# Attention probabilities transposed by DMA instead of on TensorE

## The chip, the cores and the metric

The kernel runs on all 8 cores of one Trainium2 chip. Each core computes a quarter of the sequence (1024 tokens, with 64 tokens of its neighbours on each side) of one of two batch items; the cores exchange nothing. The time is that of the slowest core on the device, in microseconds (us). The engines of a core are named as the profile names them: PE (TensorE), DVE (VectorE), ACT (ScalarE), POOL (GpSimd) and SP (SyncE, which here only issues DMAs).

## The reference

Layer normalisation, banded attention with learned sinks, and a gated feed-forward block that reads the same normalised input; the result is x + s * silu(ffn). What matters here is the attention (32 heads of 64, windows of 64, 16 sinks a head):

```python
s_band = jnp.einsum('bhnqd,bhnkd->bhnqk', Qb, Kband) * scale
s_band = jnp.where(mask, s_band, -jnp.inf)
s_sink = jnp.einsum('bhnqd,hsd->bhnqs', Qb, sinks) * scale
p = jax.nn.softmax(jnp.concatenate([s_sink, s_band], axis=-1), axis=-1)
O = jnp.einsum('bhnqs,hsd->bhnqd', p[..., :S], sinks) \
  + jnp.einsum('bhnqk,bhnkd->bhnqd', p[..., S:], Vband)
```

## The kernel before

It runs in stages, with a barrier between them: normalisation and transposing of the input, projection of q, k and v, attention, feed-forward (gate, up and down products over weights streamed from HBM), output projection and final addition.

The attention stage is a loop over 128 pairs (c, qt): c names two heads, A and B, that lie in the two halves of the partitions, and qt a tile of 128 queries. For each pair the scores of 128 queries against 16 sinks and 256 keys go to psA and psB (p3_emit_scores, three matmuls a head, L542 to L547). VectorE takes their maxima (L597, L598). ScalarE forms the exponentials into pA_bf and pB_bf (bf16, 128 queries on the partitions by 272 columns) and their sums (L620, L623). VectorE inverts the sums and scales the probabilities (L601 to L605). For the product with v the probabilities must have the keys on the partitions, so TensorE transposes them in six pieces into ps_tp: two of 128 x 128 and one of 128 x 16 (sinks) a head (p3_emit_tp, L556 to L561). VectorE copies them to SBUF, the wide pieces to pt_sb (L608, L609) and the sinks' to pts_sb (L610, L611). Six matmuls give the output (p3_emit_av, L573 to L577), and ScalarE evicts it to o_buf (L629, L631). After every eighth pair SP stores o_buf to DRAM (p3_sync). Buffers are double.

The order is written out by hand. TensorE has: scores of pairs 0 and 1, then for each i the transposes of i, the output of i, the scores of i + 2. ScalarE has for each i the exponentials of i and then the evictions of i; VectorE has the maxima, the scalings and the copies of i. The engines meet through three counting semaphores: TS is raised by TensorE, VS by VectorE, SS by ScalarE. `ts_tp[i]`, `vs_nm[i]` (scaled), `vs_pt[i]` (copied), `ts_av[i]` and `ss_oe[i]` (evicted) are their values for pair i. DMAs have semaphores of their own, wrapped by the class Slots, whose `dma` (L37) issues every DMA. The feed-forward stage's weights are loaded by POOL, which waits for the last store of the attention stage.

Of the kernel before, what the change touches and what calls it, by code (L numbers as in the profile page):

```python
# [8 lines left out]
BF16 = mybir.dt.bfloat16  # L9
# [10 lines left out]
NT_OWN = TOK // 128  # L20
DH = 64
NH = 32
NS = 16
# [64 lines left out]
def build_program2():  # L88
    nc = bass.Bass("TRN2", target_bir_lowering=False)
# [20 lines left out]
    d_oscr = nc.dram_tensor("o_scr", [16, 128, 1024], BF16, kind="Internal").ap()  # L110
# [10 lines left out]
    with ExitStack() as glob:  # L121
        eg = glob.enter_context
        ctx = Ctx(nc, glob)
# [6 lines left out]
        id_bf = eg(nc.sbuf_tensor("id_bf", [128, 128], BF16))  # L130
# [140 lines left out]
        with ExitStack() as sA:  # L271
# [209 lines left out]
            o_buf = [ea(nc.sbuf_tensor(f"o_buf{i}", [128, 1024], BF16)) for i in range(2)]  # L481
            pA_bf = [ea(nc.sbuf_tensor(f"pA_bf{i}", [128, 272], BF16)) for i in range(2)]
            pB_bf = [ea(nc.sbuf_tensor(f"pB_bf{i}", [128, 272], BF16)) for i in range(2)]
            pt_sb = [ea(nc.sbuf_tensor(f"pt_sb{i}", [128, 512], BF16)) for i in range(2)]
            pts_sb = [ea(nc.sbuf_tensor(f"pts_sb{i}", [NS, 256], BF16)) for i in range(2)]
# [6 lines left out]
            OS = Slots(nc, glob, "os", 2)  # L492
            OS_outer[0] = OS

            pairs = [(c, qt) for c in range(16) for qt in range(NT_OWN)]
            NP3 = len(pairs)
# [4 lines left out]
            vs_nm = [0] * NP3  # L501
            ts_tp = [0] * NP3
            vs_pt = [0] * NP3
            ts_av = [0] * NP3
            ss_oe = [0] * NP3
            ostok = [None] * 16
# [17 lines left out]
            for i in range(NP3):  # L524
# [5 lines left out]
                c, qt = pairs[i]  # L530
# [19 lines left out]
            def p3_emit_tp(t, i):  # L550
                ctx.wait(t, "VS", vs_nm[i])
                if i >= 2:
                    ctx.wait(t, "VS", vs_pt[i - 2])
                pt = ps_tp[i % 2]
                pa, pb = pA_bf[i % 2], pB_bf[i % 2]
                t.transpose(pt[:, 0:128], pa[:, NS:NS + 128], id_bf[:])  # L556
                t.transpose(pt[:, 128:256], pa[:, NS + 128:NS + 256], id_bf[:])
                t.transpose(pt[0:NS, 256:384], pa[:, 0:NS], id_bf[:])
                t.transpose(pt[:, 384:512], pb[:, NS:NS + 128], id_bf[:])
                t.transpose(pt[:, 512:640], pb[:, NS + 128:NS + 256], id_bf[:])  # L560
                ins = t.transpose(pt[0:NS, 640:768], pb[:, 0:NS], id_bf[:])  # L561
                ctx.inc(ins, "TS")

            def p3_emit_av(t, i):
                c, qt = pairs[i]
                ctx.wait(t, "VS", vs_pt[i])
                if i >= 1:
                    ctx.wait(t, "SS", ss_oe[i - 1])
                for hh in range(2):
                    h = 2 * c + hh  # L570
                    pav = ps_oA if hh == 0 else ps_oB
                    co = hh * 256
                    t.matmul(pav[:], v_t[:, qt, h * 64:(h + 1) * 64],  # L573
                             pt_sb[i % 2][:, co:co + 128], start=True, stop=False)
                    t.matmul(pav[:], v_t[:, qt + 1, h * 64:(h + 1) * 64],
                             pt_sb[i % 2][:, co + 128:co + 256], start=False, stop=False)
                    ins = t.matmul(pav[:], sinkn_bf[:, h * 64:(h + 1) * 64],  # L577
                                   pts_sb[i % 2][:, hh * 128:hh * 128 + 128],
                                   start=False, stop=True)
                ctx.inc(ins, "TS")  # L580

            def p3_tensor(t):
                MS.wait_all(t)
                for kind, i in tseq:
                    if kind == "sc":
                        if i >= 2:
                            ctx.wait(t, "SS", ss_ex[i - 2])
                        p3_emit_scores(t, i)
                    elif kind == "tp":
                        p3_emit_tp(t, i)  # L590
                    else:
                        p3_emit_av(t, i)

            def p3_vector(v):
                for i in range(NP3):
                    ctx.wait(v, "TS", ts_sc[i])
                    v.reduce_max(nmA[i % 2][:], psA[i % 2][:], axis=AX, negate=True)  # L597
                    ctx.inc(v.reduce_max(nmB[i % 2][:], psB[i % 2][:], axis=AX,  # L598
                                         negate=True), "VS")
                    ctx.wait(v, "SS", ss_ex[i])  # L600
                    v.reciprocal(rcA[i % 2][:], rsA[i % 2][:])  # L601
                    v.reciprocal(rcB[i % 2][:], rsB[i % 2][:])
                    v.drain()
                    v.tensor_scalar_mul(pA_bf[i % 2][:], pA_bf[i % 2][:], rcA[i % 2][:])  # L604
                    ctx.inc(v.tensor_scalar_mul(pB_bf[i % 2][:], pB_bf[i % 2][:],  # L605
                                                rcB[i % 2][:]), "VS")
                    ctx.wait(v, "TS", ts_tp[i])
                    v.tensor_copy(pt_sb[i % 2][:, 0:256], ps_tp[i % 2][:, 0:256])  # L608
                    v.tensor_copy(pt_sb[i % 2][:, 256:512], ps_tp[i % 2][:, 384:640])  # L609
                    v.tensor_copy(pts_sb[i % 2][:, 0:128], ps_tp[i % 2][0:NS, 256:384])  # L610
                    ctx.inc(v.tensor_copy(pts_sb[i % 2][:, 128:256],  # L611
                                          ps_tp[i % 2][0:NS, 640:768]), "VS")

            def p3_scalar(sc):
                for i in range(NP3):
                    c, qt = pairs[i]
                    ctx.wait(sc, "VS", vs_mx[i])
                    if i >= 2:
                        ctx.wait(sc, "TS", ts_tp[i - 2])
                    sc.activation(pA_bf[i % 2][:], psA[i % 2][:], AF.Exp,  # L620
                                  bias=nmA[i % 2][:], scale=1.0,
                                  accum_out=rsA[i % 2][:])
                    ctx.inc(sc.activation(pB_bf[i % 2][:], psB[i % 2][:], AF.Exp,  # L623
                                          bias=nmB[i % 2][:], scale=1.0,
                                          accum_out=rsB[i % 2][:]), "SS")
                    ctx.wait(sc, "TS", ts_av[i])
                    if qt == 0 and c >= 2:
                        OS.wait(sc, ostok[c - 2])
                    sc.activation(o_buf[c % 2][0:64, qt * 128:(qt + 1) * 128],  # L629
                                  ps_oA[:], AF.Copy)  # L630
                    ctx.inc(sc.activation(o_buf[c % 2][64:128, qt * 128:(qt + 1) * 128],  # L631
                                          ps_oB[:], AF.Copy), "SS")

            def p3_sync(s):
                for c in range(16):
                    last_i = c * NT_OWN + (NT_OWN - 1)
                    ctx.wait(s, "SS", ss_oe[last_i])
                    tok = OS.dma(s, d_oscr[c], o_buf[c % 2][:], c % 2)
                    assert tok == ostok[c]

            with ExitStack() as sP3:
                psA = [sP3.enter_context(nc.psum_tensor(f"psA{i}", [128, 272], F32))
                       for i in range(2)]
                psB = [sP3.enter_context(nc.psum_tensor(f"psB{i}", [128, 272], F32))
                       for i in range(2)]
                ps_tp = [sP3.enter_context(nc.psum_tensor(f"ps_tp{i}", [128, 768], BF16))
                         for i in range(2)]
                ps_oA = sP3.enter_context(nc.psum_tensor("ps_oA", [64, 128], F32))
                ps_oB = sP3.enter_context(nc.psum_tensor("ps_oB", [64, 128], F32))
                block.tensor(p3_tensor)  # L650
                block.vector(p3_vector)
                block.scalar(p3_scalar)
                block.sync(p3_sync)
                assert ctx.cnt["TS"] == cTS and ctx.cnt["VS"] == cVS
                assert ctx.cnt["SS"] == cSS
# [425 lines left out]
```

## Time and profile before

| | us |
|---|---|
| median of 3 runs | 3245.32 |
| lowest and highest | 3132.2, 3301.79 |
| the profiled execution | 3131.45 |
| its span, slowest core (core 1) | 3129.9 |
| spans of the 8 cores | 3076.9 to 3129.9 |
| PE busy | 2464.7 (79%) |
| DVE busy | 801.7 (26%) |
| ACT busy | 536.9 (17%) |
| POOL busy | 136.8 (4%) |

The profile is one execution. A line such as "1260.04 0.28 PE ps_oA L573" in the chain of work that ended last says that from 1260.04 us on, for 0.28 us, the chain ran through the matmul of line 573 that writes ps_oA; "issue" in it is time in which an engine waited for nothing that the profile shows. An instruction that overlaps the one before it is counted in the chain only from where the former ends, so its figure there can be smaller than its duration.

### The profile page before, as it was taken

To read this page: it belongs to the slowest core of one execution; us is meant where nothing else is said; L and a number is where in the kernel's file an instruction comes from. 1 tells how busy PE (TensorE), PEld (TensorE's weight loads), DVE (VectorE), ACT (ScalarE), POOL (GpSimd) and SP (SyncE) were. 2 spreads that over 40 slices of the span, in tenths; PEclk is the share of its full clock that TensorE was granted. 3 is DMA by queue.
4 is the path that set the end of the run, shared out by engine and by line. 5 is a ranking of instruction groups with operands and counts; after the bars stand their busy time and mean duration, and the time that the engine had idled before them with its cause. 6 is when DMAs were issued, how large, how long until landed. Compare 5 with 4: busy or idle time off the path is not lost.

```text
span 3129.9 us, 32762 instructions; the slowest of 8 cores (3076.9 to 3129.9 us)
## 1 busy us (share of the span) xinstructions
PE 2464.7 (79%) x11816; PEld 1126.9 (36%) x11816; DVE 801.7 (26%) x2289; ACT 536.9 (17%) x1362; POOL 136.8 (4%) x259
## 2 busy tenths in 40 slices
PE   2387776995555555555599999999999999999796
PEld 1133222772222222222244444444444444444343
DVE  4344333002333333333203121120303121211224
ACT  3244333212222222222100000000000000000010
POOL 0000000000000000000010000101010100000000
PEclk9999888995555555555599999999999999999895
DMA  2233113221000000000254353617152443524445
GB/s 96 76 54 51 30 34 54 41 41 13 4 7 4 7 4 7 4 7 7 39 86 68 68 94 54 108 33 117 26 96 52 75 87 60 102 48 88 115 75 188
DMA packets 50747, 174.03 MB, mean 56 GB/s; under 512 B 9872, under 2 KB 11040, under 8 KB 46368
## 3 DMA queue, kind: packets, MB, share of 16 engines
q0 software_dynamic: 41616, 135.04, 25.4%
q1 hardware_dynamic: 8976, 36.91, 3.4%
q8 instruction: 100, 1.64, 0.2%
q14 instruction: 55, 0.45, 0.1%
HBM read 294.36 MB, written 12.58 MB: 98 GB/s over the span
## 4 chain that ended last, share of the span: by engine, by line
PE 59%; ACT 11%; DVE 11%; DMA 9%; issue 7%; DVEq 1%; POOL 1%; ACTq 0%; SPq 0%; POOLq 0%
PE ps_d L773 15%; PE ps_g L747 11%; PE ps_u L759 11%; DMA wd_ib<-wd_pack 6%; PE ps_v L424 4%; PE ps_s L911 3%; PE ps_qk L355 3%; ACT pA_bf L620 2%; ACT pB_bf L623 2%; DVE t L388 1%; DVE m L391 1%; ACT t2sw L372 1%; DVE pA_bf L604 1%; ACT t2sw L371 1%; ACT t2sw L369 1%
## 5 line engine op out<-in xcount | busy, mean ns | idle before, releaser
L773 PE MATMUL ps_d<-h_ib,wd_ib 128*128 128x512 bf16 x2048 | 458.3, 388 | 35.5 <-DMA wd_ib<-wd_pack 35.5
L747 PE MATMUL ps_g<-xn_f,gbuf 128*128 128x512 bf16 x2048 | 465.1, 380 | 10.3 <-DMA gbuf<-wgu_pack 10.3
L759 PE MATMUL ps_u<-xn_f,ubuf 128*128 128x512 bf16 x2048 | 462.9, 379 | 0.0
L355 PE MATMUL ps_qk<-xn_f,wbuf 128*128 128x512 bf16 (+1 forms) x1280 | 285.4, 381 | 121.2 <-DVE k_f L393 74.9
L773 PEld LDWEIGHTS ps_d<-h_ib,wd_ib 128*128 128x128 bf16 x2048 | 203.6, 100 | 290.0 <-issue 58.8
L798 DVE TENSOR_TENSOR h_ib<-tg,ps_u 128x512 bf16<-128x512 f32 x128 | 88.0, 688 | 811.5 <-PE ps_u L759 811.5
L747 PEld LDWEIGHTS ps_g<-xn_f,gbuf 128*128 128x128 bf16 x2048 | 200.8, 98 | 253.5 <-issue 13.3
L788 ACT ACTIVATE tg<-ps_g 128x512 f32<-128x512 f32 x128 | 76.4, 597 | 1238.4 <-PE ps_g L747 1238.4
L759 PEld LDWEIGHTS ps_u<-xn_f,ubuf 128*128 128x128 bf16 x2048 | 200.4, 98 | 241.6
L808 DVE TENSOR_TENSOR g_sb<-g_sb,ps_d 128x512 f32<-128x512 f32 x224 | 154.0, 687 | 275.6 <-PE ps_d L773 275.6
L355 PEld LDWEIGHTS ps_qk<-xn_f,wbuf 128*128 128x128 bf16 x1280 | 118.6, 104 | 273.8 <-issue 189.4
L556 PE MATMUL ps_tp<-id_bf,pA_bf 128*128 128x128 bf16 x128 | 34.0, 266 | 194.9 <-DVE pB_bf L605 194.9
L573 PE MATMUL ps_oA<-pt_sb,v_t 128*64 128x128 bf16 x128 | 36.4, 284 | 146.3 <-DVE pts_sb L611 146.3
L424 PE MATMUL ps_v<-vbuf,xn_f 128*128 128x256 bf16 x1152 | 139.6, 275 | 2.8 <-ACT v_t L436 2.8
L629 ACT ACTIVATE o_buf<-ps_oA 64x128 bf16<-64x128 f32 x128 | 34.7, 271 | 606.2 <-PE ps_oB L577 606.2
L911 PE MATMUL ps_s<-o_sb,wobuf 128*128 128x512 bf16 x512 | 112.3, 382 | 21.4 <-DMA o_sb<-o_scr 20.8
L424 PEld LDWEIGHTS ps_v<-vbuf,xn_f 128*128 128x128 bf16 x1152 | 107.5, 98 | 23.6 <-issue 3.0
L37 POOL DMA_DIRECT2D gbuf<-wgu_pack x64 | 33.9, 530 | 1852.3 <-PE ps_g L747 1014.5
L601 DVE RECIPROCAL rcA<-rsA 128x1 f32<-128x1 f32 x128 | 20.9, 163 | 339.5 <-ACT pB_bf L623 339.5
L223 PE MATMUL ps_tr<-id_bf,xn_bf 128*128 128x128 bf16 x144 | 29.1, 264 | 95.9 <-ACT xn_bf L212 74.4
L556 PEld LDWEIGHTS ps_tp<-id_bf,pA_bf 128*128 128x128 bf16 x128 | 13.3, 104 | 228.7 <-issue 228.7
L597 DVE TENSOR_REDUCE nmA<-psA 128x1 f32<-128x272 f32 x128 | 53.7, 419 | 160.1 <-PE psB L547 160.1
(104 smaller groups left out, 2206.4 us busy)
## 6 DMA issues: line engine op xcount, KB each, us to landing
gbuf<-wgu_pack POOLq DMA_DIRECT2D x64, 512.0 KB, 6.1
ubuf<-wgu_pack POOLq DMA_DIRECT2D x64, 512.0 KB, 5.9
wd_ib<-wd_pack POOLq DMA_DIRECT2D x64, 512.0 KB, 18.1
u_buf<-u_ext SPq DMA_DIRECT2D x17, 1024.0 KB, 6.8
wbuf<-wqkv_pack POOLq DMA_DIRECT2D x32, 512.0 KB, 5.1
vbuf<-v_pack POOLq DMA_DIRECT2D x8, 1024.0 KB, 8.4
wobuf<-wo_pack POOLq DMA_DIRECT2D x16, 512.0 KB, 5.1
out<-out_buf SPq DMA_DIRECT2D x8, 1024.0 KB, 4.7
```

The costliest lines, as they stand in the source:

```text
L355: t.matmul(p[:, 0:ln], wbuf[oc % 2][:, kc * 128:(kc + 1) * 128], src[:, kc, :], start=(kc == 0), stop=False)
L424: t.matmul(p[:], xn_f[:, kc, tt * 128:(tt + 1) * 128], vbuf[gp % 2][:, kc * 256:(kc + 1) * 256], start=(kc == 0), stop=False)
L597: v.reduce_max(nmA[i % 2][:], psA[i % 2][:], axis=AX, negate=True)
L620: sc.activation(pA_bf[i % 2][:], psA[i % 2][:], AF.Exp, bias=nmA[i % 2][:], scale=1.0, accum_out=rsA[i % 2][:])
L623: ctx.inc(sc.activation(pB_bf[i % 2][:], psB[i % 2][:], AF.Exp, bias=nmB[i % 2][:], scale=1.0, accum_out=rsB[i % 2][:]), "SS")
L747: ins = t.matmul(pg[:], gbuf[ic % 2][:, kc * 128:(kc + 1) * 128], xn_f[:, kc, HALO + tsx * 512:HALO + (tsx + 1) * 512], start=(kc == 0), s ...
L759: ins = t.matmul(pu[:], ubuf[ic % 2][:, kc * 128:(kc + 1) * 128], xn_f[:, kc, HALO + tsx * 512:HALO + (tsx + 1) * 512], start=(kc == 0), s ...
L773: ins = t.matmul(pd[:], wd_ib[:, ic, oc * 128:(oc + 1) * 128], h_ib[:, ic, tsx * 512:(tsx + 1) * 512], start=(ic == 0), stop=(ic == 7))
L788: ctx.inc(sc.activation(tg[gi % 2][:], ps_g[gi % 2][:], AF.Silu), "SS")
L798: ctx.inc(v.tensor_mul(h_ib[:, ic, tsx * 512:(tsx + 1) * 512], tg[gi % 2][:], ps_u[gi % 2][:]), "VS")
L808: ins = v.tensor_add(dst, dst, ps_d[j % 2][:])
L911: ins = t.matmul(p[:], wobuf[oc % 2][:, kc * 128:(kc + 1) * 128], o_sb[:, kc, tsx * 512:(tsx + 1) * 512], start=(kc == 0), stop=(kc == 15))
```

## The change

The wide transposes leave TensorE and become DMAs. In p3_emit_tp only the two sink pieces are left, and ps_tp shrinks to 16 x 256. VectorE copies only those two. SP's p3_sync, which had only the stores, now waits in every pair for the scaled probabilities and for the output matmuls of two pairs back, and issues four `dma_start_transpose` of 128 x 128 bf16 each, from pA_bf and pB_bf straight to pt_sb, both in SBUF. Each raises the semaphore of its buffer (PT, one for each of the two buffers) by 16. TensorE waits for 64 more on it before the output matmuls, and ScalarE before it overwrites pA_bf and pB_bf two pairs later. The store of every eighth pair stands behind that pair's transposes in SP's order.

```diff
--- before.py
+++ after.py
@@ -553,17 +553,14 @@
                     ctx.wait(t, "VS", vs_pt[i - 2])
                 pt = ps_tp[i % 2]
                 pa, pb = pA_bf[i % 2], pB_bf[i % 2]
-                t.transpose(pt[:, 0:128], pa[:, NS:NS + 128], id_bf[:])
-                t.transpose(pt[:, 128:256], pa[:, NS + 128:NS + 256], id_bf[:])
-                t.transpose(pt[0:NS, 256:384], pa[:, 0:NS], id_bf[:])
-                t.transpose(pt[:, 384:512], pb[:, NS:NS + 128], id_bf[:])
-                t.transpose(pt[:, 512:640], pb[:, NS + 128:NS + 256], id_bf[:])
-                ins = t.transpose(pt[0:NS, 640:768], pb[:, 0:NS], id_bf[:])
+                t.transpose(pt[:, 0:128], pa[:, 0:NS], id_bf[:])
+                ins = t.transpose(pt[:, 128:256], pb[:, 0:NS], id_bf[:])
                 ctx.inc(ins, "TS")
 
             def p3_emit_av(t, i):
                 c, qt = pairs[i]
                 ctx.wait(t, "VS", vs_pt[i])
+                PT.wait(t, pttok[i])
                 if i >= 1:
                     ctx.wait(t, "SS", ss_oe[i - 1])
                 for hh in range(2):
@@ -605,11 +602,9 @@
                     ctx.inc(v.tensor_scalar_mul(pB_bf[i % 2][:], pB_bf[i % 2][:],
                                                 rcB[i % 2][:]), "VS")
                     ctx.wait(v, "TS", ts_tp[i])
-                    v.tensor_copy(pt_sb[i % 2][:, 0:256], ps_tp[i % 2][:, 0:256])
-                    v.tensor_copy(pt_sb[i % 2][:, 256:512], ps_tp[i % 2][:, 384:640])
-                    v.tensor_copy(pts_sb[i % 2][:, 0:128], ps_tp[i % 2][0:NS, 256:384])
+                    v.tensor_copy(pts_sb[i % 2][:, 0:128], ps_tp[i % 2][:, 0:128])
                     ctx.inc(v.tensor_copy(pts_sb[i % 2][:, 128:256],
-                                          ps_tp[i % 2][0:NS, 640:768]), "VS")
+                                          ps_tp[i % 2][:, 128:256]), "VS")
 
             def p3_scalar(sc):
                 for i in range(NP3):
@@ -617,6 +612,7 @@
                     ctx.wait(sc, "VS", vs_mx[i])
                     if i >= 2:
                         ctx.wait(sc, "TS", ts_tp[i - 2])
+                        PT.wait(sc, pttok[i - 2])
                     sc.activation(pA_bf[i % 2][:], psA[i % 2][:], AF.Exp,
                                   bias=nmA[i % 2][:], scale=1.0,
                                   accum_out=rsA[i % 2][:])
@@ -631,19 +627,43 @@
                     ctx.inc(sc.activation(o_buf[c % 2][64:128, qt * 128:(qt + 1) * 128],
                                           ps_oB[:], AF.Copy), "SS")
 
+            PT = Slots(nc, glob, "pt", 2)
+            pttok = [None] * NP3
+            ptc = [0, 0]
+            for i in range(NP3):
+                for _ in range(4):
+                    ptc[i % 2] += 16
+                pttok[i] = (i % 2, ptc[i % 2])
+
             def p3_sync(s):
-                for c in range(16):
-                    last_i = c * NT_OWN + (NT_OWN - 1)
-                    ctx.wait(s, "SS", ss_oe[last_i])
-                    tok = OS.dma(s, d_oscr[c], o_buf[c % 2][:], c % 2)
-                    assert tok == ostok[c]
+                next_store = 0
+                for i in range(NP3):
+                    c, qt = pairs[i]
+                    ctx.wait(s, "VS", vs_nm[i])
+                    if i >= 2:
+                        ctx.wait(s, "TS", ts_av[i - 2])
+                    pa, pb = pA_bf[i % 2], pB_bf[i % 2]
+                    dst = pt_sb[i % 2]
+                    s.dma_start_transpose(dst[:, 0:128], pa[:, NS:NS + 128]).then_inc(
+                        PT.sems[i % 2], 16)
+                    s.dma_start_transpose(dst[:, 128:256], pa[:, NS + 128:NS + 256]).then_inc(
+                        PT.sems[i % 2], 16)
+                    s.dma_start_transpose(dst[:, 256:384], pb[:, NS:NS + 128]).then_inc(
+                        PT.sems[i % 2], 16)
+                    s.dma_start_transpose(dst[:, 384:512], pb[:, NS + 128:NS + 256]).then_inc(
+                        PT.sems[i % 2], 16)
+                    PT.cnt[i % 2] += 64
+                    if qt == NT_OWN - 1:
+                        ctx.wait(s, "SS", ss_oe[i])
+                        tok = OS.dma(s, d_oscr[c], o_buf[c % 2][:], c % 2)
+                        assert tok == ostok[c]
 
             with ExitStack() as sP3:
                 psA = [sP3.enter_context(nc.psum_tensor(f"psA{i}", [128, 272], F32))
                        for i in range(2)]
                 psB = [sP3.enter_context(nc.psum_tensor(f"psB{i}", [128, 272], F32))
                        for i in range(2)]
-                ps_tp = [sP3.enter_context(nc.psum_tensor(f"ps_tp{i}", [128, 768], BF16))
+                ps_tp = [sP3.enter_context(nc.psum_tensor(f"ps_tp{i}", [NS, 256], BF16))
                          for i in range(2)]
                 ps_oA = sP3.enter_context(nc.psum_tensor("ps_oA", [64, 128], F32))
                 ps_oB = sP3.enter_context(nc.psum_tensor("ps_oB", [64, 128], F32))
```

## Rows read from the trace of the kernel before

**Rows 1.** Stretches: PE, PEld, DVE, ACT, POOL busy us (instructions); granted clock; DMA share, GB/s.

```profile
723.45:1535.60 812.15, 473.20 (x2292) 192.87 (x2292) 274.13 (x1274) 202.24 (x764) 0.00 (x0) 0.50 0.01 5
...
1545.20:2926.60 1381.40, 1344.46 (x6144) 604.84 (x6144) 264.11 (x384) 78.25 (x130) 99.43 (x189) 0.98 0.42 73
```

**Rows 2.** Line 556: count, duration ns min/median/max, first and last start in us.

```profile
L556 PE MATMUL ps_tp<-id_bf,pA_bf x128: 262/266/266, 723.5 to 1531.5; 128*128 128x128 bf16 x128
```

**Rows 3.** Chain that ended last, one pair: start us, us on it, what.

```profile
1253.74 0.29 PE ps_oA L573
...
1255.06 0.07 ACT o_buf L629
...
1255.64 0.58 ACT pA_bf L620 x2
...
1257.38 0.21 DVE pB_bf L605
1257.59 0.24 issue
1257.83 0.27 PE ps_tp L556
...
1259.05 0.15 DVE pt_sb L608
...
1259.66 0.14 DVE pts_sb L611
1259.80 0.24 issue
1260.04 0.28 PE ps_oA L573
```

**Rows 4.** The same chain at the attention stage's end.

```profile
1535.27 0.28 ACT o_buf L631
...
1535.61 2.03 DMA o_scr<-o_buf
...
1545.10 0.14 issue
1545.23 1.01 PE ps_g L747 x2
```

**Rows 5.** Order of time on SP's queue: start us, duration us, what is issued.

```profile
125.43 0.33 SPq L37 DMA_DIRECT2D cq_t<-cq  x1
125.81 0.42 SPq L37 DMA_DIRECT2D sq_t<-sq  x1
126.28 0.42 SPq L37 DMA_DIRECT2D ck_t<-ck  x1
126.74 0.43 SPq L37 DMA_DIRECT2D sk_t<-sk  x1
```

**Rows 6.** Order of time on POOL: issue of a load in small pieces.

```profile
709.36 0.63 POOL L37 DMA_DIRECT2D sinkn_bf<-sinks_n  x1
```

**Rows 7.** DMA issues: count, KB each, median us from issue to landing.

```profile
o_scr<-o_buf SPq DMA_DIRECT2D x16, 256.0 KB, 2.0
...
sinkt_bf<-sinks_t POOLq DMA_DIRECT2D x2, 64.0 KB, 4.0
id_f<-ident SPq DMA_DIRECT2D x1, 64.0 KB, 1.8
...
consts_sb<-consts SPq DMA_DIRECT2D x1, 2.0 KB, 1.8
```

**Rows 8.** SP's issues in the attention stage (first start us, time to the last's end).

```profile
771.92 764.01 SPq L37 DMA_DIRECT2D o_scr<-o_buf  x16
```

**Rows 9.** DMA busy tenths in 40 slices of 771.90 to 773.00 us.

```profile
DMA  0000000000000000000000000000013795597995
```

**Rows 10.** DMA busy tenths in 40 slices of 773.00 to 775.00 us.

```profile
DMA  9799997942200000000000000000000000000000
```

**Rows 11.** DMA queue 0 from 706 to 710.5 us: packets, MB, share of 16 engines.

```profile
q0 software_dynamic: 2389, 0.08, 82.7%
```

## The prediction

> **What bounds the kernel now.** I looked first at the spans of all cores. They lie between 3076.9 and 3129.9 us, and both dies have a clock of 0.833, so the slowest core speaks for all. Then I looked at the page's slices, which show a stretch of about ten slices, from about 720 to 1540 us, in which TensorE is half busy and its clock is down. Busy times by stretch give it exactly [rows 1]: from 723.45 to 1535.60 us TensorE is busy 473.20 of 812.15 us, VectorE 274.13, ScalarE 202.24, and the 16 DMA engines 1% of the time. The granted clock is 0.50, the lower of the two levels (1.2 GHz). In the feed-forward stretch behind it, it is 0.98, near the upper one. That first stretch is the attention loop that the diff edits. No engine is full in it and no transfer is, so it is bound by a chain of waits.
>
> The first transposes (L556) of the 128 pairs start from 723.5 to 1531.5 us [rows 2]; 808.0 / 127 is 6.36 us a pair. The chain that ended last shows what a pair consists of [rows 3]: the output matmuls start at 1253.74 and those of the next pair at 1260.04, 6.30 us later. In between come, one behind the other: six output matmuls, two evictions on ScalarE, two exponentials (from 1255.64), two reciprocals and two scalings on VectorE (to 1257.59), six transposes on TensorE (from 1257.83), four copies on VectorE (1259.05 to 1259.80), and the next output matmuls at 1260.04. The exponentials of a pair stand behind the evictions of the pair before in ScalarE's order, so nothing of the next pair's softmax runs ahead: each microsecond added between scaling and output matmul is added 128 times.
>
> **The change, part by part.** The piece that is replaced runs from the end of the scaling, 1257.38 + 0.21 = 1257.59, to the output matmul at 1260.04: 2.45 us [rows 3]. The other 3.85 us of the pair stay. I call the new length of this piece D.
>
> *Removed:* four of six transposes on TensorE and the two wide copies (L608, L609). *Kept:* the two transposes of the sink columns and two small copies. They start 0.24 us behind the scaling as now and are through in well under 2.45 us, since they are a subset of what takes 2.45 us today. They run beside the DMAs, so I cost them at nothing; if the DMAs were through at once, they would be the chain. VectorE's maxima of the next pair move ahead of the output matmul; they aren't on the chain today, so that gives nothing. TensorE's clock is at its lower level already and TensorE only gets less to do, so I let every matmul time stand and the feed-forward stage start as before.
>
> *Added:* SP waits for the scaling, issues four transposing DMAs of 32 KB (128 x 128 bf16) from SBUF to SBUF, and TensorE waits for all four before the output matmuls. Its terms:
>
> - SP's start behind the engine that it waits for: the eviction L631 ends at 1535.27 + 0.28 = 1535.55, SP's store starts at 1535.61: 0.06 us [rows 4].
> - Three issue spacings ahead of the fourth. Four plain loads stand back to back on SP at 125.43, 125.81, 126.28 and 126.74 us: 1.31 us for three, 0.44 each [rows 5]. The trace has no transposing DMA. The dearest issue near it is POOL's of a load in small pieces, 0.63 us [rows 6]. That is another queue's way of making descriptors, but a transpose is also cut into small pieces, so I take 0.63, which makes 1.89; the low end is 1.31.
> - The landing of the fourth, from its issue. The store of 256 KB takes 2.03 us [rows 4] and 16 of them have a median of 2.0. Loads of 64 KB and of only 2 KB take 1.8, so size is hardly in it; a 64 KB load in small pieces takes 4.0 [rows 7]. A transpose has smaller pieces than the store (rows of 256 bytes) and larger ones than that load (64 bytes), and a reordering on top. I take 2.7, nearer to the store; the ends are 2.03 and 4.0.
> - TensorE's start behind a DMA: 0.14 us, rounded to 0.13 where the chain counts to the matmul [rows 4].
>
> D is then 0.06 + 1.89 + 2.7 + 0.13 = 4.78 us. That is 2.33 us more than 2.45, and times 128 it is 298 us. At the low end, D is 0.06 + 1.31 + 2.03 + 0.13 = 3.53, +1.08 a pair, +138 us. At the high end, with 0.63 and 4.0, D is 6.08, +3.63, +465 us.
>
> *Stores.* SP's 16 stores of o_buf now stand in the order between the transposes. The first store issues at 771.92 [rows 8], just as ScalarE begins the next pair's exponentials; from there to the end of the next scaling it is 1257.59 - 1255.64 = 1.95 us [rows 3]. The next issue could follow after 0.44 us [rows 5], so the store is out of the way; without that cover it would cost 16 x 0.44 = 7 us. SP's wait for the output matmuls two pairs back is always met by then. ScalarE's new wait, for the transposes two pairs back, is met too, since those output matmuls have run. What stands behind TensorE's new wait are the output matmuls and the scores two pairs on, whose buffers are a pair ahead. POOL's feed-forward loads wait for the last store and so start later by just what the loop grows.
>
> The profiled execution is 3131.45 us (its span 3129.9), and I sum against it: 3131 + 298 = 3429 us. The median of the runs shown is 3245.32 and the lowest 3132.2, so the profiled one is among the fastest; I forecast for executions like it, and the range has room for a median that is some tens of us above.
>
> The Trainium skill, Advanced Engine Details and Errata, section X-Bar Transpose (TRN2), says that a transposing DMA on this chip is as fast as a plain one. By it D would be the low end above; no row here shows one.
>
> **Rivals.**
>
> *1. The four transposes run one behind the other.* In the sum they overlap and only their issues are apart. If the path that reorders takes one at a time and holds it for t, D is 0.06 + 4t + 0.13 at least. For t there is only a bound: a whole landing each, 2.03 us [rows 4], which gives D = 8.31, +5.86 a pair, +750 us: 3881 us. The middle between 0.44 (the spacing of plain issues, below which it has no effect) and 2.03 is 1.24; it gives D = 5.15, +346 us, 3477 us. It overtakes my forecast's D of 4.78 from t = 1.15 us on. For it: all four use the same engines and one queue. Against it: pieces pass quickly. 2389 small packets took 82.7% of 16 engines over 4.5 us [rows 11], that is 59.5 us of engine time or 25 ns each, and a transpose has 128 rows, 8 for an engine, 0.2 us.
> The Trainium skill, VectorE: DVE Perf Modes, section The three transpose paths, gives 1309 ns for a 128 x 128 bf16 transpose by DMA and 390 ns on TensorE. If that is what each holds the path for, D would be an estimated 5.4 us and the time about 3510 us, between forecast and rival. TensorE's own figure isn't met here: one such transpose (L556) has a median of 266 ns [rows 2].
>
> *2. It isn't slower.* What is transposed is 32 KB and never leaves SBUF, and four transposes on TensorE and two copies are gone from the chain. The first store's packets begin at about 772.70 and end at about 773.55 [rows 9, 10], so of the 2.03 us that follow its issue at 771.92 [rows 8] some 0.85 are data; 1.2 us are left for a transfer without any. With spacings of 0.44, D is 0.06 + 1.31 + 1.2 + 0.13 = 2.70, +0.25 a pair, +32 us: 3163 us, which can't be told from no change. It decides at D = 2.94, where 0.49 x 128 is 2%; for a gain of 2%, D would have to be 1.96, which four issues of 0.44 leave only 0.46 for. Against it: a load of 2 KB, almost no data, still took 1.8 us [rows 7].
>
> *3. The transposes move single elements.* 16384 elements at 25 ns over 16 engines [rows 11] are 25.6 us for one, 102 us a pair, and the kernel would take over 16000 us. A milder form, a piece of 32 bytes at a time (1024 pieces, 1.6 us each, in series), gives D = 0.06 + 6.4 + 1.2 + 0.13 = 7.8 us and falls together with rival 1. For the single elements only the layout speaks: source neighbours land on different partitions.
>
> **How the numbers follow.** The forecast's mechanism (issues apart, landings overlapping, D from 3.53 to 6.08): 3269 to 3596 us, chance 0.60. Rival 1, t from 1.15 to 2.03, 3430 to 3881 us: 0.25, of which two fifths for t below 1.4. Rival 3 or anything beyond: 0.07. Rival 2: 0.08, of which 0.02 for faster. The range of 3265 to 3890 us takes in the first two, 0.85. A change of under about 2% can't be told from none, so: faster 0.02, within 2% 0.06, slower 0.92. The likeliest case gives 3429 us.
>
> **What the profile after would show.** The period of L573 or of the first transpose: 8.6 us a pair instead of 6.3, with the stretch at 1110 us instead of 812. The output matmul's idle time should be ended by a DMA, about 3.5 us or more of it a pair. In SP's order, four issues a pair 0.44 to 0.63 us apart. If they are 1.2 us or more apart, or the landing grows from the first transpose to the fourth, it is rival 1 (or the issue itself is the bound, which my 0.63 would have missed). Evictions, exponentials and scalings should have their old durations and the feed-forward stretch its 1381 us. If the output matmul's wait is still ended by the small copies (now L607), rival 2 holds. The forecast is wrong above all if the issue or the landing of a transposing DMA is unlike a plain one's: each 0.1 us in a spacing is worth 3 x 0.1 x 128 = 38 us, each 0.1 us in the landing 13 us.

## The result, and the profile after

The changed kernel is slower. Its median is 3628.17 us over 9 runs (lowest 3610.22); the ratio to the kernel before is 1.159, with a 95% interval of 1.155 to 1.163. The profiled execution took 3610.22 us, 479 us more than the profiled one of before (3131.45). The forecast was 3429 us: the right direction and the right place, but 298 us of growth instead of 479. In some executions of both kernels, and in all three of the one with eight DMAs below, the cores of one die were slowed, which lifts the plain medians (before: 3242.11 over 10 runs); the ratios, and the times quoted below for every kernel but that one, leave those executions out.

The waits of the changed kernel on its slowest core (who waited for whom: us in total, times, longest) have one new row at TensorE. It answers to the 146.3 us that the output matmul waited for VectorE's copies before:

```profile
PE ps_oA L570 <- DMA pt_sb<-pB_bf: 747.2, 128, 6.9
```

The lines that answer to [rows 1] are busy times by stretch of the changed kernel, the attention loop and the feed-forward stage (PE, PEld, DVE, ACT, POOL, granted clock, DMA share and GB/s):

```profile
729.00:2049.60 1320.60, 378.75 (x1780) 151.95 (x1780) 224.09 (x1022) 201.49 (x764) 0.00 (x0) 0.50 0.07 16
2058.00:3405.00 1347.00, 1332.81 (x6144) 601.59 (x6144) 263.49 (x384) 77.70 (x129) 99.44 (x188) 1.00 0.42 75
```

The loop grew from 812 to 1321 us with less work in it, at the same granted clock of 0.50. The 16 DMA engines are busy 7% of it, so it isn't the data.

The chain that ended last, through one pair of the changed kernel, answers to [rows 3] (start us, us on the chain, what):

```profile
1257.14 1.10 SPq L647
1258.23 0.04 issue
1258.28 1.23 SPq L649
1259.51 0.04 issue
1259.55 1.23 SPq L651
1260.78 0.04 issue
1260.83 2.33 DMA pt_sb<-pB_bf
1263.16 0.40 issue
1263.55 0.28 PE ps_oA L570
```

The scaling of this pair ends at 1257.03. SP starts 0.11 us later, holds its queue for 1.10 us with the first transposing DMA and for 1.23 us with each further one, and can start the fourth only at 1260.83. That one lands 2.33 us later. From scaling to output matmul it is 1263.55 - 1257.03 = 6.52 us, against 2.45 us before. The first of the four already holds the queue for 1.10 us, when those of the pair before have long landed (the output matmul of that pair started at 1253.18): so the hold belongs to the issue itself, and waiting for an earlier transpose can be at most the 0.13 us by which the others are dearer.

Over the whole loop: the tile pt_sb of the changed kernel lists, for each instruction that writes or reads it, the duration (min/median/max ns) and the first and last start:

```profile
L647 SPq DMA_TRANSPOSE pt_sb<-pA_bf x128: 1093/1095/1174, 730.3 to 2041.0; - x128
L649 SPq DMA_TRANSPOSE pt_sb<-pA_bf x128: 1214/1232/2350, 731.6 to 2042.1; - x128
L651 SPq DMA_TRANSPOSE pt_sb<-pB_bf x128: 1095/1232/2301, 732.8 to 2043.4; - x128
L653 SPq DMA_TRANSPOSE pt_sb<-pB_bf x128: 1226/1232/1236, 734.1 to 2045.7; - x128
...
L570 PE MATMUL ps_oA<-pt_sb,v_t x128: 283/286/288, 736.6 to 2048.3; 128*64 128x128 bf16 x128
...
DMA to landing us min/median/max: 2.2/2.3/4.9
```

The output matmul's first and last starts give (2048.3 - 736.6) / 127 = 10.33 us a pair, 3.97 more than the 6.36 of [rows 2], so 508 us in 128 pairs. Most pairs take 10.2 to 10.3 us; single ones take up to 11.3, some of them where an issue is held for about 2 us (the largest values of L649 and L651). The rest of the difference lies outside the loop: the first scaling ends at 730.24 instead of 723.35 us (the masks' load took 12.6 instead of 7.6 us), +7, and the feed-forward stretch took 1347 instead of 1381 us, -34. These are two different cores: the slowest of before (core 1) lost 35.5 us to late wd_ib loads, the slowest of after (core 6) 11.8 us; and TensorE was busy 11.7 us less in the stretch, at a granted clock of 1.00 instead of 0.98. 508 + 7 - 34 = 481, measured 479.

### The profile page after: what moved, and what is told of

The parts are those of the page before. It is cut to its first block, busy times and chain, and to the rows that moved or that the text cites. A ratio compares the mean times of both kernels' runs of the same rounds, so it can differ in the third digit from the quotient of the medians.

```text
span 3608.7 us, 32502 instructions; the slowest of 8 cores (3575.1 to 3608.7 us)
## 1 busy us (share of the span) xinstructions
PE 2360.8 (65%) x11304; PEld 1082.4 (30%) x11304; DVE 752.3 (21%) x2033; ACT 536.0 (15%) x1362; POOL 136.8 (4%) x259
## 3 DMA queue, kind: packets, MB, share of 16 engines
q1 hardware_dynamic: 90896, 53.75, 5.2%
## 4 chain that ended last, share of the span: by engine, by line
PE 49%; DMA 14%; SPq 13%; ACT 10%; DVE 8%; issue 5%; DVEq 1%; POOL 1%; ACTq 0%; POOLq 0%
PE ps_d L793 12%; PE ps_g L767 10%; PE ps_u L779 10%; DMA pt_sb<-pB_bf 8%; SPq L649 5%; SPq L651 4%; SPq L647 4%; PE ps_v L424 4%; DMA wd_ib<-wd_pack 3%; PE ps_s L931 3%; PE ps_qk L355 3%; ACT pA_bf L616 2%; ACT pB_bf L619 2%; DVE t L388 1%; DVE m L391 1%
## 5 line engine op out<-in xcount | busy, mean ns | idle before, releaser
L793 PE MATMUL ps_d<-h_ib,wd_ib 128*128 128x512 bf16 x2048 | 446.0, 381 | 13.9 <-DMA wd_ib<-wd_pack 11.8
L570 PEld LDWEIGHTS ps_oA<-pt_sb,v_t 128*64 128x64 bf16 x128 | 16.3, 127 | 779.2 <-issue 779.2
L556 PE MATMUL ps_tp<-id_bf,pA_bf 128*16 128x128 bf16 x128 | 33.9, 265 | 196.2 <-DVE pB_bf L602 196.2
L424 PEld LDWEIGHTS ps_v<-vbuf,xn_f 128*128 128x128 bf16 x1152 | 107.4, 98 | 23.7 <-issue 3.0
```

The lines of the kernel that those rows point to most:

```text
L424: t.matmul(p[:], xn_f[:, kc, tt * 128:(tt + 1) * 128], vbuf[gp % 2][:, kc * 256:(kc + 1) * 256], start=(kc == 0), stop=False)
L793: ins = t.matmul(pd[:], wd_ib[:, ic, oc * 128:(oc + 1) * 128], h_ib[:, ic, tsx * 512:(tsx + 1) * 512], start=(ic == 0), stop=(ic == 7))
```

## The experiments

The first question was what makes SP's issue three times as dear as a plain DMA's 0.44 us. Theory F says that the time is fixed for each transposing DMA, whatever its size. Theory T says that it grows with the number of 16 x 128 tiles in it. The second question was whether the chain of waits, and not an engine or a queue, makes the loop what it is in both kernels.

### Two wide DMAs for four

```diff
-  four s.dma_start_transpose of 128 x 128
+  s.dma_start_transpose(dst[:, 0:256].rearrange("p (a b) -> p a b", a=2), pa[:, NS:NS + 256])
+  s.dma_start_transpose(dst[:, 256:512].rearrange("p (a b) -> p a b", a=2), pb[:, NS:NS + 256])
```

> The changed kernel with the same data in two transposing DMAs of 128 x 256 for a pair instead of four of 128 x 128. Theory F, the time that a transposing DMA holds SP's queue (1.23 us) is fixed for each DMA: both still take about 1.2 us, one spacing of 1.27 us ahead of the last instead of three, the pair falls from 10.33 to about 7.8 us, the kernel to about 3290 us. Theory T, it grows with the tiles of 16 x 128 that a DMA holds (8 in the changed kernel, 16 here): each takes 2 to 2.5 us, the pair stays between 9.8 and 10.4 us, the kernel at about 3600 us.

Measured: 3322.62 us; a pair is (1726.6 - 730.4) / 127 = 7.84 us. The tile pt_sb in this kernel:

```profile
L647 SPq DMA_TRANSPOSE pt_sb<-pA_bf x128: 1152/1154/1401, 726.6 to 1722.7; - x128
L650 SPq DMA_TRANSPOSE pt_sb<-pB_bf x128: 1188/1216/2584, 727.9 to 1723.8; - x128
L570 PE MATMUL ps_oA<-pt_sb,v_t x128: 283/284/287, 730.4 to 1726.6; 128*64 128x128 bf16 x128
```

A DMA with twice the data holds SP's queue for about as long as before, 1.15 to 1.22 us on this core (core 1) and 1.17 to 1.25 us on the even ones; T wanted 2 us or more. Issues are a little dearer on even cores (see the last section), so the price of a spacing is taken between even ones: on core 6 a pair of this kernel is (1732.1 - 732.4) / 127 = 7.87 us, and (10.33 - 7.87) / 2 is 1.23 us for each spacing that is gone. F holds, T falls.

### One tile instead of eight

```diff
-  s.dma_start_transpose(dst[:, 0:128], pa[:, NS:NS + 128])            (and three more)
+  s.dma_start_transpose(dst[:, 0:16], pa[0:16, NS:NS + 128])          (and three more)
```

> The changed kernel with four transposing DMAs of one tile (16 x 128) each for a pair instead of eight tiles each; the other seven eighths of the probabilities are left out (zeros stand there), so its output is not the reference's. Theory F: each still holds SP's queue for 1.1 to 1.2 us, the pair stays at 10.3 us and the kernel at 3610 us. Theory T: the issue falls towards the 0.44 us spacing of a plain DMA, the pair to about 7.5 us, the kernel to about 3250 us.

Measured: 3620.47 us in the profiled execution and (2046.4 - 738.3) / 127 = 10.30 us a pair, with an eighth of the data:

```profile
L650 SPq DMA_TRANSPOSE pt_sb<-pA_bf x128: 1085/1087/1178, 732.1 to 2040.0; - x128
L652 SPq DMA_TRANSPOSE pt_sb<-pA_bf x128: 1197/1224/2356, 733.3 to 2041.1; - x128
...
DMA to landing us min/median/max: 2.2/2.3/3.5
```

With an eighth of the data the issue falls by only 0.01 us (1.09 and 1.22 against 1.10 and 1.23), and the landing doesn't. This is F from the other side.

### Plain copies in the same place

```diff
-  s.dma_start_transpose(dst[:, 0:128], pa[:, NS:NS + 128])            (and three more)
+  s.dma_start(dst[:, 0:128], pa[:, NS:NS + 128])                      (and three more)
```

> The changed kernel with each transposing DMA replaced by a plain copy of the same 128 x 128 block, SBUF to SBUF; the transposition of the wide blocks is left out, so its output is not the reference's. This prices the low end of the prediction. If only the transposing makes SP's issue dear: spacings of 0.44 us, landing of 1.6 to 2.0 us, D of about 3.5 us (from scaling to output matmul), the pair 7.3 us, the kernel 3260 us. If any short DMA in this place costs that much (its wait, or the SBUF source): spacing 1.2 us and 3550 us or more.

Measured: 3350.05 us, (1739.9 - 734.0) / 127 = 7.92 us a pair. The first lines are the tile pt_sb, the others one pair in order of time (start us, duration us):

```profile
L647 SPq DMA_DIRECT2D pt_sb<-pA_bf x128: 464/465/521, 730.2 to 1735.9; - x128
L649 SPq DMA_DIRECT2D pt_sb<-pA_bf x128: 574/587/873, 730.7 to 1736.4; - x128
...
DMA to landing us min/median/max: 1.7/1.8/3.0
```

```profile
1259.32 0.28 DVE L602 TENSOR_SCALAR pB_bf<-pB_bf,rcB 128x272 bf16<-128x272 bf16 x1
1259.73 0.46 SPq L647 DMA_DIRECT2D pt_sb<-pA_bf  x1
1260.24 0.58 SPq L649 DMA_DIRECT2D pt_sb<-pA_bf  x1
1260.87 0.58 SPq L651 DMA_DIRECT2D pt_sb<-pB_bf  x1
1261.49 0.59 SPq L653 DMA_DIRECT2D pt_sb<-pB_bf  x1
...
1263.58 0.28 PE L570 MATMUL ps_oA<-pt_sb,v_t 128*64 128x128 bf16 x1 [3.36 <-DMA pt_sb<-pB_bf]
```

Between the two cases of the expectation: spacings of 0.51, 0.63 and 0.62 us, 1.76 us for three, dearer than the 1.31 of the loads in [rows 5], and a landing of 1.8 us. From scaling to output matmul it is 3.98 us. So my middle value of 0.63 us for a spacing is what a plain SBUF to SBUF copy costs in this place; transposing adds 0.64 us to each spacing and 0.5 us to the landing. A landing is counted from the start of the issue. From the issue's end on it is 2.3 - 1.23 = 1.1 us for a transposing DMA and 1.8 - 0.59 = 1.2 us for a plain one: so what the transposing adds lies in the issue alone, and the landing is later because the issue is longer. Of the loop's +508 us, about (7.92 - 6.36) x 128 = 200 us would be there with plain copies, and about 308 us are the transposing.

### Half of the transposes back on TensorE

```diff
-  s.dma_start_transpose(dst[:, 256:384], pb[:, NS:NS + 128])  and its neighbour
+  t.transpose(pt[:, 256:384], pb[:, NS:NS + 128], id_bf[:])   and its neighbour
+  v.tensor_copy(pt_sb[i % 2][:, 256:512], ps_tp[i % 2][:, 256:512])
```

> The changed kernel with head B's two wide blocks transposed on TensorE and copied by VectorE as before, head A's two by DMA. If each issue costs 1.27 us on the chain: D falls by two spacings, 2.54 us, from 6.5 to 4.0 us, the pair to 7.8 us, the kernel to about 3285 us, and the output matmul still waits for a DMA. If the landing, not the issues, were what counts, the pair would stay above 9 us and the kernel above 3450 us.

Measured: 3319.14 us, (1723.4 - 730.8) / 127 = 7.82 us a pair; the output matmul still waits for a DMA:

```profile
PE ps_oA L572 <- DMA pt_sb<-pA_bf: 370.2, 128, 4.0
```

Two issues less are 10.33 - 7.82 = 2.51 us less, as two wide DMAs for four were 2.46 us less (core 6). Half of the data or all of it in two DMAs comes to the same.

### Eight DMAs for four

```diff
-  s.dma_start_transpose(dst[:, 0:128], pa[:, NS:NS + 128])            (and three more)
+  s.dma_start_transpose(dst[:, 0:64], pa[0:64, NS:NS + 128])
+  s.dma_start_transpose(dst[:, 64:128], pa[64:128, NS:NS + 128])      (and six more)
```

> The changed kernel with each transposing DMA cut into two of 64 rows by 128 columns, eight for a pair with the same data. Theory F (issue time fixed for each DMA): four more spacings of 1.27 us, the pair from 10.33 to about 15.4 us, the kernel to about 4260 us. Theory T (by the tile): the pair stays near 10.4 us.

Measured: 4341.56 us in the profiled execution; the rows are of core 5 (span 4217.4 us). The last of its eight issues and the output matmul:

```profile
L661 SPq DMA_TRANSPOSE pt_sb<-pB_bf x128: 1197/1198/1204, 736.3 to 2665.9; - x128
L570 PE MATMUL ps_oA<-pt_sb,v_t x128: 283/286/287, 738.8 to 2668.6; 128*64 128x128 bf16 x128
```

A pair is (2668.6 - 738.8) / 127 = 15.20 us; in the changed kernel an odd core needs 10.24 us (core 7: 733.1 to 2033.9). Four more issues are 4.96 us, 1.24 us each. From one tile to sixteen in a DMA, and from two to eight DMAs a pair, the time follows the number of DMAs, and their size hardly matters.

### One DMA a pair

Head B's sink columns go behind its keys, so that the 512 wide columns of both heads are one run in memory:

```diff
-  pA_bf, pB_bf: two tensors [128, 272], each sinks then keys
+  pAB_bf: one tensor [128, 544]: sinks A, keys A, keys B, sinks B
+  s.dma_start_transpose(dst[:].rearrange("p (a b) -> p a b", a=4), pAB_bf[i % 2][:, NS:NS + 512])
```

> The changed kernel with one transposing DMA of 128 x 512 for a pair (head B's sink columns moved behind its keys so that the source is one run; the computation is the same). Theory F (issue time fixed for each DMA): D is one landing and two wake-ups, about 2.8 us, the pair 6.7 us, the kernel about 3180 us. Theory T (issue time by the tile, 0.15 us each, 32 tiles here): the issue takes about 4.9 us, D stays at 6.3 us or more, the kernel at 3590 us.

> The changed kernel with one transposing DMA of 128 x 512 a pair, timed again in rounds against the kernel before. In the one profiled execution a pair took 6.77 us against 6.36 of before, +0.41 x 128 = 52 us, so a ratio of 1.015 to 1.025 is expected: the change's loss almost gone, but no gain.

Measured: 3198.81 us in one execution, (1590.4 - 730.0) / 127 = 6.77 us a pair. The chain of this kernel, one pair (start us, us on it, what):

```profile
1105.08 0.21 DVE pAB_bf L607
...
1105.41 2.42 DMA pt_sb<-pAB_bf
1107.84 0.24 issue
1108.08 0.29 PE ps_oA L575
```

No issue spacing is left. From scaling (1105.29) to output matmul it is 2.79 us, 0.34 more than the 2.45 us of TensorE and VectorE. The issue of 1.19 us is within the 2.42 us of landing; T wanted 4.9 us for it. The size isn't quite without effect: the first issue of a pair takes 1.087, 1.095, 1.169 and 1.190 us for DMAs of 1, 8, 16 and 32 tiles (medians on even cores), 0.10 us more for 32 times the data. In further runs the kernel took 3175.25 to 3198.22 us against 3128.95 and 3134.63 of before: a ratio of about 1.016. The loss is nearly gone and there is no gain. It also shows the limit of the theory that only SP's issues matter: with one DMA the path is still one landing long.

### The order changed alone

Theory: the loop is bound by its chain. Then the transposes' path is expensive only because nothing else is done meanwhile. I moved the work of neighbouring pairs into each other, first with all transposes on TensorE as before:

```diff
 for i in range(NP3):
     tseq.append(("tp", i))
-    tseq.append(("av", i))
+    if i >= 1: tseq.append(("av", i - 1))
     if i + 2 < NP3: tseq.append(("sc", i + 2))
+ VectorE: scale(i), maxima(i + 1), copies(i)
+ ScalarE: exponentials(i), evictions(i - 2)
```

> The kernel before with its order changed alone: TensorE runs the output matmuls of a pair behind the transposes of the next one, ScalarE the exponentials of a pair ahead of the evictions of two pairs back, VectorE the maxima of the next pair ahead of the copies. If the attention loop is bound by the chain of waits and not by an engine, the pair falls from 6.36 us to what TensorE is busy at the lower clock, 473 / 128 = 3.7 us, the stretch from 812 to about 480 us, the kernel to about 2800 us, lower if the clock rises. If an engine or the waits between engines bind it, it stays above 3000 us.

Measured: ratio 0.891 (0.887 to 0.895); runs of 2783.15 to 2796.45 us; (1191.5 - 731.9) / 127 = 3.62 us a pair. From 800 to 1100 us its chain is TensorE alone. The first lines are a part of that chain, from the scores of one pair over the transposes to the output of another; the second are the busy times of a stretch of the loop:

```profile
1003.23 0.23 PE psB L562
1003.45 0.22 PE ps_tp L571
...
1004.31 0.21 PE ps_tp L576
1004.52 0.24 PE ps_oA L588
```

```profile
800.00:1100.00 300.00, 300.00 (x1488) 125.18 (x1488) 185.43 (x826) 130.85 (x496) 0.00 (x0) 0.50 0.03 10
```

TensorE is busy 300.00 of 300 us. The old order was bound by its chain: same instructions, another order, 335 to 350 us less.

### The new order with the DMAs

> The changed kernel with the same new order, so that a pair's transposing DMAs fly while the next pair's softmax runs. If the loss of the change is the length of the DMA path on the chain and SP's queue is the next bound: the pair takes four spacings, about 5.15 us, less than the 6.36 of before; the kernel about 2990 us, faster than before by 4 to 5% but slower than the same order with transposes on TensorE. If the DMAs' latency can't be covered (buffers of the probabilities are given back only when they land), the pair is 8 us or more and the kernel above 3300 us.

The edit is that of the section above, made to the changed kernel; SP's stores also move back by two pairs. Measured: ratio 0.951 (0.949 to 0.952), 2973.88 to 2978.91 us; (1405.2 - 733.5) / 127 = 5.29 us a pair. For most of the loop its chain runs from one issue to the next on SP's queue:

```profile
1003.26 1.13 SPq L672
1004.38 0.04 issue
1004.43 1.23 SPq L674
1005.66 0.04 issue
1005.70 1.23 SPq L676
...
1006.97 2.35 DMA pt_sb<-pB_bf
```

The DMAs' latency is covered: a pair takes 5.29 us, less than the 6.52 us between one pair's scaling and its output matmul in the changed kernel. What can't be covered is the queue: four issues of about 1.27 us are 5.1 us a pair, and most pairs take 5.10 us. The mean is higher because a pair with a store in SP's order takes 5.73 us and because 18 of the 512 issues are held for 1.3 to 2.4 us; why, no run shows. Now and then the profile's chain leaves the queue for a landing, as in the last line. But that path has room: the landing, at 1009.32, lets the exponentials of two pairs on begin, and their scaling ends at 1011.35, 2 us before SP's queue is free at 1013.32. The same four DMAs that cost 16% in the old order are part of a kernel that is 5% faster than before in the new one, and 6.6% slower than the new order alone (2977 against about 2791 us).

### The new order with one DMA

> The new order with one transposing DMA of 128 x 512 a pair. Theory F: SP is no bound any more (1.2 us a pair), the pair is bound by TensorE with less to do than before or by the softmax chain, 3.3 to 4 us, the kernel 2760 to 2850 us. Theory T: SP's issue stays near 4.9 us a pair and the kernel at about 2960 to 2990 us.

> The new order with one transposing DMA of 128 x 512 a pair, timed in rounds. In one profiled execution a pair took 3.19 us; (3.19 - 6.36) x 128 is -406 us, a ratio of about 0.87, below the 0.891 of the same order with all transposes on TensorE: with the DMA covered, what it takes from TensorE counts.

Measured: 2729.95 us in one execution, (1137.7 - 732.0) / 127 = 3.19 us a pair, a little below what theory F had given; in further runs it took 2723.74, 2732.11 and 2734.63 us, a ratio of about 0.872 to the 3128.95 and 3134.63 us of before. Busy times of the same stretch of the loop:

```profile
800.00:1100.00 300.00, 274.99 (x1312) 111.24 (x1311) 165.10 (x750) 139.88 (x563) 0.00 (x0) 0.50 0.25 52
```

This is the fastest version, about 2% under the new order with all transposes on TensorE. The two ratios, 0.872 and 0.891, come from separate sets of runs; the periods of a pair, 3.19 and 3.62 us, bear them out (0.43 x 128 = 55 us of the 60 between the times). TensorE is busy 274.99 / 300 x 3.19 = 2.92 us a pair now, 0.70 less than the 3.62 of before, and isn't full any more. Only 0.43 of the 0.70 are gained, since the loop is bound by a chain again. Part of it, over two pairs in 6.24 us:

```profile
999.95 0.25 PE ps_oA L590
...
1002.99 0.44 DVE nmB L616
...
1003.62 0.52 ACT pAB_bf L640 x2
...
1005.36 0.21 DVE pAB_bf L624
...
1006.19 0.25 PE ps_oA L590
```

It goes from an output matmul over the scores, the maxima, the exponentials, the scaling and the small transposes to the output matmul two pairs on. A few long landings, up to 5.1 us, add to the mean.

## Why the prediction was right in direction and short in size

*The chain bounds the loop, and each microsecond in the replaced piece counts 128 times.* Right. 3.97 us more a pair by the period, 4.07 us in the piece itself in the pair shown. The new order without any other edit (ratio 0.891) shows that it was the chain.

*What is kept lies beside the DMAs; other terms stay.* Right. In the pair of the changed kernel the exponentials still take 0.58 and 0.48 us on the chain, and no small copy ends the output matmul's wait. The clock was 0.50 in both loops. The stores cost nothing that shows: the growth is explained without them.

*SP's start behind the scaling, 0.06 us.* 0.11 us; SP waits for two semaphores there.

*Three issue spacings, 1.89 us.* This is the step that failed. They are 1.14 + 1.27 + 1.28 = 3.69 us, 1.80 us a pair or 230 us too low. I had bounded the spacing by rows of plain DMAs, 0.44 us on SP and 0.63 us on POOL, and taken both ends from them; no row held a transposing DMA. That my value met plain copies in this place almost exactly (0.51 to 0.63 us) shows what was missing: a price for the transposing itself, 0.64 us for each instruction, nearly whatever its size. The range held the time only because rival 1's end was in it. An operation that no row shows needed an upper bound from something other than its cheapest relatives, or a wider middle.

*The landing, 2.7 us.* 2.33 us, 0.37 too high. Its size independence was right: 2.3 us for one tile, 2.4 us for 32. The reordering that I had added to it isn't there: what exceeds a plain landing (0.5 us) is the longer issue with which it begins.

*TensorE's start behind a DMA, 0.13 us.* 0.24 us in the pair before the one shown, 0.39 us in the latter.

Put together: 4.78 + 0.05 + 1.80 - 0.37 + 0.26 = 6.52 us.

*Rival 1, the transposes run one behind the other on the path that reorders.* In effect near, in mechanism wrong. Spacings are 1.27 us, about the middle value of t that I gave it (1.24), and its outlook of issues 1.2 us or more apart came true. But it is SP's queue that is held, not the path of the data: the first issue of a pair, with no transpose in flight, holds it for 1.10 us already, and the landing is 2.3 us in the median for head A's two as for head B's two and hardly grows with the data. No run issued from a second queue, which would show whether two queues are held independently.

```profile
pt_sb<-pA_bf SPq DMA_TRANSPOSE x256, 2.3
pt_sb<-pB_bf SPq DMA_TRANSPOSE x256, 2.3
```

(DMA issues of the changed kernel: count, median us to landing.) The prediction had named this alternative only in brackets, as the issue itself being the bound. The Trainium skill's figure of 1309 ns for a 128 x 128 block (VectorE: DVE Perf Modes, The three transpose paths) lies close to the spacing of 1.27 us, and the estimate for the kernel worked out from it, 3510 us, was nearer than mine. Here the trace agrees with the number but not with a price by the block: a 128 x 512 transpose held the queue for 1.19 us. The Trainium skill's rule that a transposing DMA is as fast as a plain one (Advanced Engine Details and Errata, X-Bar Transpose (TRN2)) agrees with the trace only behind the issue (1.1 us against 1.2 us of a plain copy to the landing); the issue itself takes 1.23 instead of 0.59 us, and that makes about 308 of the loop's 508 us.

*Rival 2, not slower,* fell: 2.33 us of landing, with no part of it saved by the small size. *Rival 3, single elements,* fell: the hardware queue's packets rose from 8976 to 90896 in the whole kernel, 160 for each of the 512 transposing DMAs, where the rival needed 16384, or 1024 in its milder form.

*The sum outside the loop.* I left 0 for it; it was -27 us, mostly by another slowest core with 23.7 us less of late wd_ib loads. That is the size of what separates cores here, not an effect of the change that the runs show.

## What to carry to other kernels

Before a DMA replaces engine work inside a serial loop, count its instructions and not its bytes: each held the issuing queue for 1.2 us here and each last one took 2.3 us to land, so pack a step's transposes into one DMA, or leave them on TensorE. If the loop is a chain in which no engine is full, reorder it first. The order alone gave 11%. In the old order the four DMAs cost 16% and one DMA a pair 1.6%; in the new order four still cost 6.6%, and one gave 2% on top.

## What the runs showed of the hardware that I had not expected

- A transposing DMA from SBUF to SBUF held SP's queue for 1.07 to 1.25 us and landed 2.3 to 2.4 us after its issue began, for 4 KB as for 128 KB (medians). A plain copy of 32 KB in the same place held it for 0.46 to 0.60 us and landed in 1.8 us. The first of a group is cheaper by about 0.13 us than those behind it.
- The issues are a little dearer on even cores (1.232 us on cores 0, 2, 4 and 6) than on odd ones (1.202 us on cores 1, 3, 5 and 7; this is core 7):

```profile
L653 SPq DMA_TRANSPOSE pt_sb<-pB_bf x128: 1194/1202/1208, 730.7 to 2031.2; - x128
```

  The loop takes 1311.7 us on core 6 and 1300.8 on core 7, 11 us of the 26 us by which core 6's span exceeds core 7's. Why, no run shows.
- With TensorE busy 300.00 of 300 us in the reordered loop, the granted clock stayed at 0.50, the lower level (1.2 GHz), as in the loop full of waits; in the feed-forward stretch it was 0.98 to 1.00. So the waits alone don't explain the low clock of this loop. What would raise it there stays open; it wasn't tried.
